# A GNN layer on one core: seven edge products per tile instead of eight, and another order of VectorE's and GpSimd's work in the first tiles

## The chip, the cores and the metric

The kernel runs on one core of one Trainium2 chip. The metric is the device time of one execution in microseconds (us); lower is better. Three timed runs of the kernel before gave a median of 1362.57 us.

## The reference

Only what sets the shape of the work is kept.

```python
def reference(x, src, dst, edge_attr_64, W1, b1, W2, b2):
    # x: 50000 x 256, edge_attr_64: 25000 x 64, dst sorted; W1: 320 x 512, W2: 512 x 256
    h = jnp.maximum(_layernorm(x, axis=-1), 0.0)
    agg = segment_sum(edge_attr_64, dst, num_segments=50000)
    counts = segment_sum(ones(25000), dst, num_segments=50000)
    agg = agg / jnp.maximum(counts, 1.0)[:, None]
    combined = jnp.concatenate([agg, h], axis=1)
    hidden = jax.nn.relu(combined @ W1 + b1)
    return x + hidden @ W2 + b2
```

So each node gets the mean of its incoming edges (64 wide), beside its normalised features (256 wide), and both go through a two-layer perceptron; the result is added to x.

## The kernel before

**Tiles.** The 50000 nodes are cut into 98 tiles of 512 nodes, each of four groups of 128. All engines' instructions are written out by hand, in one program per engine, with semaphores between them. Tiles 0, 1 and the start of tile 2 are unrolled; from tile 2 to tile 95 a loop runs two tiles (`step(2i)`, `step(2i+1)`) per pass, and the last two tiles are unrolled again. Buffers of a tile come in pairs (b = 0 or 1), those after the transposition (HT, QA, QB, H1) exist once.

**Precision.** Every product is made of fp32r operands split into a high and a low part: a value is rounded to fp32r (`_hi`), and the rest is kept beside it (`_lo`). A product a·b is hi·hi + lo·hi + hi·lo.

**One tile on TensorE (PE).** `step(t)` issues, for each of the four slices m of the hidden layer, six products of 512 columns from the node features (`layer1_nodes`, L884 to L886) and two from the edge means (`layer1_means`, L893 and L894). Between m = 1 and m = 2 stand the edge products of the next tile, `edge_means(t+1)`, L873 and L874: for each group k of 128 nodes, a one-hot matrix OH (which of the 128 edges in a window goes to which of 128 nodes) is multiplied with E_hi and with E_lo, 64 columns of weights and 128 moving columns each. Both accumulate into rows 0 to 63 of the bank PA; that makes eight products. Then `layer2` issues 16 pairs (L907 with 512 columns, L909 with 256); the first six pairs need the slices m = 0 to 2 of the hidden layer, the seventh needs m = 3. In the steps of tiles 0 and 1 the edge products of the next tile stand inside `layer2`, behind the eighth pair, and not between the slices.

**What the means pass through.** ScalarE (ACT) rounds PA into QB (L587) and copies that into rows 0 to 63 of QA (L589). VectorE (DVE) writes the rest, PA − QB, into rows 64 to 127 of QA (L711, `means_low`), and the semaphore s_qlo tells TensorE that L893 may start.

**Where the other operands come from.** SyncE (SP) loads x and the edge windows: per tile, eight small transfers whose places it reads from a table of addresses (L308 into ER, L309 into DT). VectorE computes the windows' relative targets (`ends`, L651) and four one-hots (`onehot`, L813). GpSimd (POOL) scales the edges (L427, into ES), ScalarE rounds them (L576, E_hi) and GpSimd subtracts (L432, E_lo). ScalarE normalises x (L570); SP then moves the result into four quadrants with four transfers (L275, HQ, called `move`), VectorE transposes it in two halves (L699), ScalarE and VectorE split it (L582, L707). In a step VectorE transposes the first half of tile t+1 before it makes the low part of slice m = 3 of tile t (`hidden_low`, L715), which the seventh pair of `layer2` needs. At the end it makes the outputs (`residual`, L726 and L729) of each group of nodes. GpSimd adds the bias to x for a later tile (`residual_in`, L438, 128x1024).

**What sets the order.** Each engine takes its instructions strictly as written; a wait holds all behind it. SP's program in the first tiles is: windows of tile 2, `move(2)`, windows of tile 3, store of tile 0, x of tile 4, windows of tile 4, `move(3)`, store of tile 1, x of tile 5, windows of tile 5, `move(4)`. VectorE's order for tile 1 ends with: transposition of tile 2, `residual(1, 0)`, `residual(1, 1)`, `means_low(2)`, `residual(1, 2)`, `residual(1, 3)`, then `ends(3)` and `onehot(3)`. The wait that stands before the edge products of a tile on TensorE is this:

```python
pe.wait_ge(s_oh, SUB * t + SUB)   # all four one-hots of tile t
pe.wait_ge(s_elo, t + 1)          # its E_lo
```

The functions that the change touches, with the line numbers of the profile:

Of the kernel before, what the change touches and what calls it, by code (L numbers as in the profile page):

```python
# [5 lines left out]
ALU = mybir.AluOpType  # L6
ACT = mybir.ActivationFunctionType
# [7 lines left out]
P = 128  # L15
SUB = 4
# [10 lines left out]
def build(nc, x, src, dst, edge_attr, w1, b1, w2, b2, out):  # L27
# [41 lines left out]
    with ExitStack() as ctx:  # L69
        def sb(name, shape, dt=F32):  # L70
            return ctx.enter_context(nc.sbuf_tensor(name, shape, dt))
# [4 lines left out]
        def sem(name):  # L76
            return ctx.enter_context(nc.semaphore(name))
# [57 lines left out]
        rel = [sb(f"rel{b}", [P, SUB]) for b in range(2)]  # L135

        ES = [sb(f"ES{b}", [P, SUB, DE]) for b in range(2)]
        E_hi = [sb(f"E_hi{b}", [P, SUB, DE], F32R) for b in range(2)]
        E_lo = [sb(f"E_lo{b}", [P, SUB, DE], F32R) for b in range(2)]
        OH = [sb(f"OH{b}", [P, SUB, P], F32R) for b in range(2)]  # L140
        HT = sb("HT", [P, CD, TILE])
        HT_hi = sb("HT_hi", [P, CD, TILE], F32R)
# [46 lines left out]
        def groups(t):  # L189

            return range(GROUPS if isinstance(t, int) and t == TILES - 1 else SUB)
# [46 lines left out]
        s_hhi = sem("s_hhi")  # L238
        s_hlo = sem("s_hlo")
        s_qhi = sem("s_qhi")  # L240
        s_qlo = sem("s_qlo")
        s_l1 = sem("s_l1")
        s_1hi = sem("s_1hi")
# [167 lines left out]
        def _(pool):  # L411
# [17 lines left out]

            def edges_low(t, b):  # L430
                pool.wait_ge(s_ehi, t + 1)
                pool.tensor_tensor(E_lo[b][:], ES[b][:], E_hi[b][:], ALU.subtract).then_inc(s_elo, 1)  # L432

            def residual_in(t, b):

                past(pool, s_fin, SUB * (t - 1))
                pool.wait_ge(s_x[b], 16 * (t // 2 + 1) if isinstance(t, int) else 8 * t + (16 - 8 * b))
                pool.tensor_tensor(XB[b][:], X[b][:], b2_row[:].unsqueeze(1).to_broadcast([P, SUB, D]),  # L438
                                   ALU.add).then_inc(s_xb, 1)
# [97 lines left out]
            edges_low(1, 1)  # L537
            edges_scaled(2, 0)
            edges_low(2, 0)
            residual_in(2, 0)  # L540
            norm(3, 1)
            edges_scaled(3, 1)
            edges_low(3, 1)
            residual_in(3, 1)
            with pool.Fori(1, TILES // 2 - 1) as i:
                for h in range(2):
# [6 lines left out]
        @block.scalar  # L553
        def _(act):
            act.dma_start(X[0][:], x[0:TILE, :].rearrange("(j p) d -> p j d", p=P)).then_inc(s_x[0], 16)
            for q in range(QN):
                act.dma_start(w1_raw[q * QP:(q + 1) * QP, :, :],
                              w1[DE + q * QF:DE + (q + 1) * QF, :].rearrange("(c f) h -> f c h", f=QP)).then_inc(s_w[0], 16)
            act.dma_start(b2_row[:], b2.rearrange("(o d) -> o d", o=1).to_broadcast([P, D])).then_inc(s_b2, 16)

            def layernorm(t, b, js=range(SUB)):

                past(act, s_hq[b], moved(t - 2, b))
                act.wait_ge(s_norm, t + 1)
                for j in js:
                    rows, into = X[b][:, j, :], HN[b][:, j, :]
                    if isinstance(t, int) and t == 0:
                        rows = rows.rearrange("p (q c f) -> p q c f", q=QN, c=CD)
                        into = into.rearrange("p (c q f) -> p q c f", q=QN, c=CD)
                    act.activation(into, rows, ACT.Relu, bias=shift[b][:, j:j + 1],  # L570
                                   scale=rstd[b][:, j:j + 1]).then_inc(s_ln, 1)

            def edges_high(t, b):
                act.wait_ge(s_es, t + 1)
                past(act, s_sum, t - 1)
                act.activation(E_hi[b][:], ES[b][:], ACT.Copy).then_inc(s_ehi, 1)  # L576

            def transposed_high(t):
                past(act, s_l1, CH * t)
                for c in range(CD):  # L580
                    act.wait_ge(s_th, 2 * t + c + 1)
                    act.activation(HT_hi[:, c, :], turned(t, c), ACT.Copy).then_inc(s_hhi, 1)  # L582

            def means_high(t):
                past(act, s_l1, CH * t)
                act.wait_ge(s_sum, t + 1)
                act.activation(QB[0:DE, :], PA[0:DE, :], ACT.Copy).then_inc(s_qhi, 1)  # L587
                act.wait_ge(s_qhi, 2 * t + 1)
                act.activation(QA[0:DE, :], QB[0:DE, :], ACT.Copy).then_inc(s_qhi, 1)  # L589

            def hidden_high(t):
                for m in range(CH):
                    act.wait_ge(s_l1, CH * t + m + 1)
                    if m == 0:
                        past(act, s_l2, SUB * t)
                    act.activation(H1_hi[:, m, nodes(t)], bank(m)[:, nodes(t)], ACT.Relu).then_inc(s_1hi, 1)  # L596

            act.wait_ge(s_rise, 1)
            act.activation(alike[:, 1:WIDE], rise[:], ACT.Relu, bias=ones_f[0:EP, :], scale=-1.0).then_inc(s_alike, 1)
            act.wait_ge(s_w[0], 16 * QN)  # L600
            act.activation(w1_hi[:], w1_raw[:], ACT.Copy).then_inc(s_whi, 1)
            act.wait_ge(s_w[1], 32)
            act.activation(wa_hi[:], wa_raw[:], ACT.Copy).then_inc(s_whi, 1)
            act.wait_ge(s_w[2], 32)
            act.activation(b1_hi[DE:P, :], b1_raw[DE:P, :], ACT.Copy).then_inc(s_whi, 1)
            act.activation(wb_lo[64:96, :], b1_raw[64:96, :], ACT.Copy).then_inc(s_whi, 1)
            layernorm(0, 0)
            transposed_high(0)
            act.wait_ge(s_w[3], 32)
            act.activation(w2_both[:, :, 0, :], w2_raw[:], ACT.Copy).then_inc(s_whi, 1)  # L610
            layernorm(1, 1)
            edges_high(0, 0)
            means_high(0)
            hidden_high(0)
            edges_high(1, 1)
            layernorm(2, 0)
            transposed_high(1)
            means_high(1)
            edges_high(2, 0)
            hidden_high(1)  # L620
            transposed_high(2)
            means_high(2)
            layernorm(3, 1)
            edges_high(3, 1)
            with act.Fori(1, TILES // 2 - 1) as i:
                for h in range(2):
                    hidden_high(2 * i + h)
                    transposed_high(2 * i + (h + 1))
                    means_high(2 * i + (h + 1))
                    layernorm(2 * i + (h + 2), h)  # L630
                    edges_high(2 * i + (h + 2), h)
            hidden_high(TILES - 2)
            transposed_high(TILES - 1)
            means_high(TILES - 1)
            hidden_high(TILES - 1)
# [3 lines left out]
        def _(dve):  # L639
# [68 lines left out]

            def means_low(t):
                dve.wait_ge(s_qhi, 2 * t + 1)  # L710
                dve.tensor_tensor(QA[DE:P, :], PA[0:DE, :], QB[0:DE, :], ALU.subtract).then_inc(s_qlo, 1)  # L711

            def hidden_low(t, m):
                dve.wait_ge(s_1hi, CH * t + m + 1)
# [122 lines left out]
            transpose(2, 0, 0)  # L837
            transpose(2, 0, 1)
            transposed_low(2)
            residual(1, 1, 0)  # L840
            residual(1, 1, 1)
            means_low(2)
            residual(1, 1, 2)
            residual(1, 1, 3)
            ends(3, 1)
            onehot(3, 1)
            with dve.Fori(1, TILES // 2 - 1) as i:
                for h in range(2):
                    step(2 * i + h, h)
# [5 lines left out]
        def _(pe):  # L855
# [10 lines left out]
            def edge_means(t, b):  # L866
                pe.wait_ge(s_oh, SUB * t + SUB)
                pe.wait_ge(s_elo, t + 1)
                past(pe, s_qhi, 2 * t)
                past(pe, s_qlo, t)  # L870
                for k in groups(t):
                    cols = slice(k * P, (k + 1) * P)
                    pe.matmul(PA[0:DE, cols], E_hi[b][:, k, :], OH[b][:, k, :], start=(k == 0), stop=False)  # L873
                    last = pe.matmul(PA[0:DE, cols], E_lo[b][:, k, :], OH[b][:, k, :], start=False, stop=(k == groups(t)[-1]))  # L874
                last.then_inc(s_sum, 1)

            def layer1_nodes(t, m):
# [38 lines left out]
            def step(t, b, later=True):  # L916
                for m in range(CH):
                    if not (isinstance(t, int) and t == 0):
                        layer1_nodes(t, m)
                    layer1_means(t, m)  # L920
                    if m == 1 and later and not (isinstance(t, int) and t < 2):
                        edge_means(t + 1, 1 - b)
                layer2(t)

            pe.wait_ge(s_start, 1)
# [19 lines left out]
            layer1_nodes(0, 2)  # L945
            layer1_nodes(0, 3)
            edge_means(0, 0)
            pe.wait_ge(s_wlo, 2)
            pe.wait_ge(s_ones, 1)
            pe.wait_ge(s_wblo, 2)  # L950
            pe.wait_ge(s_whi, 5)
            step(0, 0)
            step(1, 1)
            with pe.Fori(1, TILES // 2 - 1) as i:
# [26 lines left out]
```

## Time and profile before

| | us |
|---|---|
| median of 3 runs | 1362.57 (1361.99 to 1363.06) |
| the profiled execution, its time | 1361.83 |
| its span, first to last instruction | 1360.0 |
| TensorE busy in it | 1333.9 |
| VectorE busy | 1194.1 |
| ScalarE busy | 695.4 |
| GpSimd busy | 539.7 |
| mean granted TensorE clock | 0.999 of full |

All times of the sections below are counted from the first instruction of the span. "Busy" of TensorE counts matmuls whose ends are modelled and overlap, so its use is better read from the distance between the starts of two matmuls than from the duration of one. "Idle before" names the time that an engine stood still before an instruction, and the engine and tile that released it.

### The profile page before, as it was taken

How to read it: one execution, taken by the hardware profiler on the slowest of the kernel's cores; microseconds unless marked ns; L12 is line 12 of the kernel's file. 1: busy time of each engine (PE TensorE's matmuls, PEld its weight loads, DVE VectorE, ACT ScalarE, POOL GpSimd, SP SyncE). 2: the span in 40 equal slices, each digit the busy share in tenths (PEclk: the TensorE clock that was granted, in tenths of full speed). 3: DMA queues.
4: the chain of work that ended last, by engine and by line, in shares of the span. 5: the costliest groups of instructions: out<-in, count | busy, mean ns of one | idle time of the engine just before them, and what ended most of it. 6: DMA issues, size and time to landing. Idle time of an engine off the chain costs nothing.

```text
span 1360.0 us, 29811 instructions
## 1 busy us (share of the span) xinstructions
PE 1333.9 (98%) x7066; PEld 1118.8 (82%) x7066; DVE 1194.1 (88%) x2961; ACT 695.4 (51%) x1281; POOL 539.7 (40%) x710
## 2 busy tenths in 40 slices
PE   4899999999999999999999999999999999999999
PEld 2688888888888888888888888888888888888887
DVE  5989898988888898989898989898889888989897
ACT  3445555555555454545454545454545454545553
POOL 6333343434343434343434343434343434343431
PEclk9999999999999999999999999999999999999999
DMA  4455555555454545454545464545454545555542
GB/s 112 111 127 120 133 121 130 126 126 130 121 132 120 132 120 133 119 136 115 140 112 143 109 147 107 145 108 143 111 141 112 139 114 137 116 135 118 133 111 74
DMA packets 422724, 168.59 MB, mean 124 GB/s; under 512 B 321188, under 2 KB 422326, under 8 KB 422712
## 3 DMA queue, kind: packets, MB, share of 16 engines
q1 hardware_dynamic: 421720, 167.28, 51.2%
q10 hardware_dynamic: 992, 1.18, 0.3%
q14 instruction: 9, 0.07, 0.0%
q8 instruction: 3, 0.05, 0.0%
HBM read 66.12 MB, written 51.40 MB: 86 GB/s over the span
## 4 chain that ended last, share of the span: by engine, by line
PE 95%; DVE 3%; DMA 1%; POOL 1%; issue 0%; ACT 0%; POOLq 0%; DVEq 0%; SPq 0%
PE P L907 26%; PE P L909 13%; PE P L884 13%; PE P L886 13%; PE P L885 13%; PE P L893 6%; PE P L894 6%; PE PA L873 2%; PE PA L874 2%; DVE H_lo L715 0%; DMA dst_w<-in_dst_dram 0%; DVE OH L813 0%; DVE below L670 0%; DVE stats L645 0%; DVE HT L699 0%
## 5 line engine op out<-in xcount | busy, mean ns | idle before, releaser
L907 PE MATMUL P<-w_both,H_hi 128*128 128x512 f32 x1564 | 557.6, 397 | 1.1 <-DVE H_lo L715 1.0
L596 ACT ACTIVATE H_hi<-P 128x512 fp32r<-128x512 f32 x392 | 233.1, 596 | 513.4 <-PE P L894 513.4
L909 PE MATMUL P<-w_both,H_lo 128*128 128x256 f32 x1564 | 439.6, 281 | 0.0
L715 DVE SCALAR_TENSOR_TENSOR H_lo<-P,H_hi 128x512 fp32r<-128x512 f32 x392 | 268.0, 685 | 113.2 <-ACT H_hi L596 103.2
L907 PEld LDWEIGHTS P<-w_both,H_hi 128*128 128x128 f32 x1564 | 293.7, 188 | 74.8 <-DVE H_lo L715 3.4
L884 PE MATMUL P<-HT_hi,w_hi 128*128 128x512 f32 (+1 forms) x784 | 314.4, 401 | 1.9 <-ACT w_both L610 1.9
L886 PE MATMUL P<-HT_hi,w_lo 128*128 128x512 f32 (+1 forms) x784 | 308.9, 394 | 0.0
L885 PE MATMUL P<-HT_lo,w_hi 128*128 128x512 f32 (+1 forms) x784 | 306.0, 390 | 0.0
L909 PEld LDWEIGHTS P<-w_both,H_lo 128*128 128x128 f32 x1564 | 293.4, 188 | 3.7
L438 POOL TENSOR_TENSOR XB<-X,b_row 128x1024 f32<-128x1024 f32 x98 | 236.8, 2416 | 135.5 <-DVE O L729 135.3
L432 POOL TENSOR_TENSOR E_lo<-ES,E_hi 128x256 fp32r<-128x256 f32 x98 | 73.2, 747 | 400.6 <-ACT E_hi L576 400.6
L699 DVE STREAM_TRANSPOSE HT<-HQ 128x512 f32<-128x512 f32 x194 | 209.3, 1080 | 0.0
L570 ACT ACTIVATE HN<-X,shift,rstd 128x256 f32<-128x256 f32 x392 | 202.4, 587 | 8.3 <-POOL shift L421 8.3
L582 ACT ACTIVATE HT_hi<-HT 128x512 fp32r<-128x512 f32 x194 | 122.9, 633 | 116.4 <-DVE HT L699 116.4
L729 DVE TENSOR_TENSOR O<-P,XB 128x256 f32<-128x256 f32 x391 | 166.0, 425 | 13.3
L886 PEld LDWEIGHTS P<-HT_hi,w_lo 128*128 128x128 f32 x784 | 147.8, 188 | 34.0
L884 PEld LDWEIGHTS P<-HT_hi,w_hi 128*128 128x128 f32 x784 | 148.2, 189 | 29.6 <-ACT w_both L610 2.3
L885 PEld LDWEIGHTS P<-HT_lo,w_hi 128*128 128x128 f32 x784 | 148.7, 190 | 25.3
L726 DVE TENSOR_TENSOR XB<-P,XB 128x256 f32<-128x256 f32 x391 | 163.5, 418 | 4.6 <-PE P L909 1.5
L893 PE MATMUL P<-QA,wa_hi 128*128 128x512 f32 x392 | 153.4, 391 | 1.6 <-POOL w_both L534 1.6
L894 PE MATMUL P<-QB,wb_lo 128*128 128x512 f32 x392 | 152.9, 390 | 0.0
L707 DVE TENSOR_TENSOR HT_lo<-HT,HT_hi 128x512 fp32r<-128x512 f32 x194 | 134.9, 695 | 15.4 <-ACT HT_hi L582 9.2
(74 smaller groups left out, 1140.0 us busy)
## 6 DMA issues: line engine op xcount, KB each, us to landing
HQ<-HN SPq DMA_DIRECT2D x388, 128.0 KB, 3.1
out_dram<-O SPq DMA_DIRECT2D x97, 512.0 KB, 3.3
X<-in_x_dram SPq DMA_DIRECT2D x96, 512.0 KB, 3.6
ER<-in_edge_attr_dram SPq DMA_DIRECT2D x392, 32.0 KB, 1.8
DT<-table_dram SPq DMA_DIRECT2D x392, 1.0 KB, 1.7
X<-in_x_dram ACTq DMA_DIRECT2D x1, 512.0 KB, 5.0
w_raw<-in_L_gnn_W_dram ACTq DMA_DIRECT2D x4, 128.0 KB, 5.2
w_raw<-in_L_gnn_W_dram SPq DMA_DIRECT2D x2, 256.0 KB, 4.0
```

Of the source, the lines that this page charges most:

```text
L438: pool.tensor_tensor(XB[b][:], X[b][:], b2_row[:].unsqueeze(1).to_broadcast([P, SUB, D]), ALU.add).then_inc(s_xb, 1)
L570: act.activation(into, rows, ACT.Relu, bias=shift[b][:, j:j + 1], scale=rstd[b][:, j:j + 1]).then_inc(s_ln, 1)
L596: act.activation(H1_hi[:, m, nodes(t)], bank(m)[:, nodes(t)], ACT.Relu).then_inc(s_1hi, 1)
L699: dve.transpose(HT[:, c, :].rearrange("p (j n k) -> p k j n", j=SUB, k=QN), HQ[b][:, :, c * QP:(c + 1) * QP].rearrange("p (k j) f -> p k j ...
L715: dve.scalar_tensor_tensor(out=H1_lo[:, m, nodes(t)], in0=bank(m)[:, nodes(t)], scalar=0.0, in1=H1_hi[:, m, nodes(t)], op0=ALU.max, op1=AL ...
L884: pe.matmul(bank(m)[:, nodes(t)], w1_hi[:, c, cols], HT_hi[:, c, nodes(t)], start=(c == 0), stop=False)
L885: pe.matmul(bank(m)[:, nodes(t)], w1_hi[:, c, cols], HT_lo[:, c, nodes(t)], start=False, stop=False)
L886: pe.matmul(bank(m)[:, nodes(t)], w1_lo[:, c, cols], HT_hi[:, c, nodes(t)], start=False, stop=False)
L893: pe.matmul(bank(m)[:, nodes(t)], wa_hi[:, cols], QA[:, nodes(t)], start=False, stop=False)
L894: pe.matmul(bank(m)[:, nodes(t)], wb_lo[:, cols], QB[:, nodes(t)], start=False, stop=True).then_inc(s_l1, 1)
L907: pe.matmul(out_bank(j)[some, :], H1_hi[:, m, rows], w2_both[:, m, :, :].rearrange("p a d -> p (a d)"), start=(m == 0), stop=False)
L909: last = pe.matmul(out_bank(j)[some, 0:D], H1_lo[:, m, rows], w2_both[:, m, 0, :], start=False, stop=(m == CH - 1))
```

## The change

**E_hi and E_lo become one tile.** E_both holds, for each group, 64 columns of the high part and next to them 64 of the low part. ScalarE and GpSimd write the two halves where they wrote the two tiles. For group 0 one product with 128 columns of weights replaces two with 64: its sum of the high part lands in rows 0 to 63 of PA and that of the low part in rows 64 to 127. The other three groups keep their two products. So a tile has seven edge products.

**The low part of group 0 is added on VectorE.** Behind L711 `means_low` gets a second instruction, over rows 64 to 127 and the 128 columns of group 0: QA = PA + QA. It waits for a new semaphore, s_qpart, which L711 raises; s_qlo is raised by the second instruction now.

**The first tiles.** GpSimd waits for the one-hots of tile 2 before `residual_in(2)`, and for those of tile 3 before `residual_in(3)`. On VectorE `ends(3)` and `onehot(3)` go ahead of all of tile 1's residuals, and `means_low(2)` goes ahead of the second. TensorE's wait for the split W2 moves from before the first use of QA to before `layer2(0)`.

```diff
-        E_hi = [sb(f"E_hi{b}", [P, SUB, DE], F32R) for b in range(2)]
-        E_lo = [sb(f"E_lo{b}", [P, SUB, DE], F32R) for b in range(2)]
+        E_both = [sb(f"E_both{b}", [P, SUB, 2, DE], F32R) for b in range(2)]
...
-                pool.tensor_tensor(E_lo[b][:], ES[b][:], E_hi[b][:], ALU.subtract).then_inc(s_elo, 1)
+                pool.tensor_tensor(E_both[b][:, :, 1, :], ES[b][:], E_both[b][:, :, 0, :], ALU.subtract).then_inc(s_elo, 1)
...
             edges_low(2, 0)
+            pool.wait_ge(s_oh, 3 * SUB)
             residual_in(2, 0)
             norm(3, 1)
             edges_scaled(3, 1)
             edges_low(3, 1)
+            pool.wait_ge(s_oh, 4 * SUB)
             residual_in(3, 1)
...
-                act.activation(E_hi[b][:], ES[b][:], ACT.Copy).then_inc(s_ehi, 1)
+                act.activation(E_both[b][:, :, 0, :], ES[b][:], ACT.Copy).then_inc(s_ehi, 1)
...
             def means_low(t):
                 dve.wait_ge(s_qhi, 2 * t + 1)
-                dve.tensor_tensor(QA[DE:P, :], PA[0:DE, :], QB[0:DE, :], ALU.subtract).then_inc(s_qlo, 1)
+                dve.tensor_tensor(QA[DE:P, :], PA[0:DE, :], QB[0:DE, :], ALU.subtract).then_inc(s_qpart, 1)
+                dve.wait_ge(s_qpart, t + 1)
+                dve.tensor_tensor(QA[DE:P, 0:P], PA[DE:P, 0:P], QA[DE:P, 0:P], ALU.add).then_inc(s_qlo, 1)
...
             transposed_low(2)
+            ends(3, 1)
+            onehot(3, 1)
             residual(1, 1, 0)
+            means_low(2)
             residual(1, 1, 1)
-            means_low(2)
             residual(1, 1, 2)
             residual(1, 1, 3)
-            ends(3, 1)
-            onehot(3, 1)
...
-                for k in groups(t):
+                pe.matmul(PA[:, 0:P], E_both[b][:, 0, :, :].rearrange("p a d -> p (a d)"), OH[b][:, 0, :],
+                          start=True, stop=True)
+                for k in groups(t)[1:]:
                     cols = slice(k * P, (k + 1) * P)
-                    pe.matmul(PA[0:DE, cols], E_hi[b][:, k, :], OH[b][:, k, :], start=(k == 0), stop=False)
-                    last = pe.matmul(PA[0:DE, cols], E_lo[b][:, k, :], OH[b][:, k, :], start=False, stop=(k == groups(t)[-1]))
+                    pe.matmul(PA[0:DE, cols], E_both[b][:, k, 0, :], OH[b][:, k, :], start=(k == 1), stop=False)
+                    last = pe.matmul(PA[0:DE, cols], E_both[b][:, k, 1, :], OH[b][:, k, :], start=False,
+                                     stop=(k == groups(t)[-1]))
...
+                if isinstance(t, int) and t == 0:
+                    pe.wait_ge(s_whi, 5)
+                    pe.wait_ge(s_wlo, 2)
                 layer2(t)
...
             edge_means(0, 0)
-            pe.wait_ge(s_wlo, 2)
             pe.wait_ge(s_ones, 1)
             pe.wait_ge(s_wblo, 2)
-            pe.wait_ge(s_whi, 5)
             step(0, 0)
```

Two places of the order, as the programs have them. The first is VectorE at the end of tile 1, from the low part of slice m = 3 on (P11 is that slice's bank; P20 and P21 hold the outputs of groups 0 and 1). Before:

```order
L715 SCALAR_TENSOR_TENSOR H1_lo<-P11,H1_hi 128x512
L699 STREAM_TRANSPOSE HT<-HQ0 128x4x128 x2
L707 TENSOR_TENSOR HT_lo<-HT,HT_hi 128x512 x2
L726 TENSOR_TENSOR XB1<-P20,XB1 128x256
L729 TENSOR_TENSOR O1<-P20,XB1 128x256
L726 TENSOR_TENSOR XB1<-P21,XB1 128x256
L729 TENSOR_TENSOR O1<-P21,XB1 128x256
L711 TENSOR_TENSOR QA<-PA,QB 64x512
```

And now, the same place of VectorE's program (its line numbers are higher by 2 to 4):

```order
L719 SCALAR_TENSOR_TENSOR H1_lo<-P11,H1_hi 128x512
L701 STREAM_TRANSPOSE HT<-HQ0 128x4x128 x2
L709 TENSOR_TENSOR HT_lo<-HT,HT_hi 128x512 x2
L653 TENSOR_TENSOR rel1<-DT1,base 128x4
L817 TENSOR_SCALAR OH1<-iota_row,rel1 128x128 x4
L730 TENSOR_TENSOR XB1<-P20,XB1 128x256
L733 TENSOR_TENSOR O1<-P20,XB1 128x256
L713 TENSOR_TENSOR QA<-PA,QB 64x512
L715 TENSOR_TENSOR QA<-PA,QA 64x128
```

The targets and the four one-hots of tile 3 stand ahead of the residuals now, one residual pair fewer stands before the subtraction into QA, and the addition over 64x128 follows it.

The second place is TensorE in the loop, from the end of slice m = 1 on (OH1 and E_hi1 are those of the next tile). Before:

```order
L893 MATMUL P13<-QA,wa_hi 128x512
L894 MATMUL P13<-QB,wb_lo 128x512
L867 ISA
L868 REGISTER_ALU
L24 REGISTER_ALU
L873 MATMUL PA<-OH1,E_hi1 64x128
L874 MATMUL PA<-OH1,E_lo1 64x128
```

And now:

```order
L900 MATMUL P13<-QA,wa_hi 128x512
L901 MATMUL P13<-QB,wb_lo 128x512
L871 ISA
L872 REGISTER_ALU
L24 REGISTER_ALU
L875 MATMUL PA<-OH1,E_both1 128x128
L879 MATMUL PA<-OH1,E_both1 64x128
L880 MATMUL PA<-OH1,E_both1 64x128
```

The product with 128 columns of weights comes first, right behind a product of 512 moving columns; six of 64 columns follow it, where eight stood.

## Rows read from the trace of the kernel before

**Rows 1.** The page: busy time of each engine, share of the span, instructions.

```profile
PE 1333.9 (98%) x7066; PEld 1118.8 (82%) x7066; DVE 1194.1 (88%) x2961; ACT 695.4 (51%) x1281; POOL 539.7 (40%) x710
```

**Rows 2.** Busy time in one steady tile (start:end, length, then each engine's).

```profile
699.38:712.91 13.53, 13.53 (x74) 11.40 (x73) 11.98 (x31) 7.06 (x15) 5.36 (x7) 1.00 0.52 126
```

**Rows 3.** Timeline (start, duration, us), TensorE and its loads around a tile's edge products.

```profile
702.23 0.39 PE L894 MATMUL P<-QB,wb_lo 128*128 128x512 f32 x1
702.45 0.22 PE L873 MATMUL PA<-OH,E_hi 128*64 128x128 f32 x1
702.46 0.14 PEld L874 LDWEIGHTS PA<-OH,E_lo 128*64 128x64 f32 x1
...
702.52 0.14 PEld L873 LDWEIGHTS PA<-OH,E_hi 128*64 128x64 f32 x1
...
702.88 0.19 PEld L884 LDWEIGHTS P<-HT_hi,w_hi 128*128 128x128 f32 x1
702.93 0.45 PE L884 MATMUL P<-HT_hi,w_hi 128*128 128x512 f32 x1
...
703.22 0.39 PE L885 MATMUL P<-HT_lo,w_hi 128*128 128x512 f32 x1
```

**Rows 4.** Timeline: VectorE's wait in a steady tile, its subtraction, TensorE's load behind it.

```profile
705.66 0.69 DVE L715 SCALAR_TENSOR_TENSOR H_lo<-P,H_hi 128x512 fp32r<-128x512 f32 x1 [1.02 <-ACT H_hi L596]
...
712.22 0.69 DVE L711 TENSOR_TENSOR QA<-PA,QB 64x512 fp32r<-64x512 f32 x1
...
713.46 0.19 PEld L893 LDWEIGHTS P<-QA,wa_hi 128*128 128x128 f32 x1
```

**Rows 5.** L711 alone (ns min/median/max, first and last start); L729 by line (busy, mean ns).

```profile
L711 DVE TENSOR_TENSOR QA<-PA,QB x98: 683/684/685, 33.5 to 1346.7; 64x512 fp32r<-64x512 f32 x98
L729 DVE TENSOR_TENSOR O<-P,XB 128x256 f32<-128x256 f32 x390 | 165.6, 425 | 13.3
```

**Rows 6.** Timeline: one-hots on VectorE, GpSimd's bias addition, tiles 2 and 3, one steady.

```profile
46.88 3.57 DVE L813 TENSOR_SCALAR OH<-iota_row,rel 128x128 fp32r<-128x128 f32 x4
47.60 2.46 DVE L813 TENSOR_SCALAR OH<-iota_row,rel 128x128 fp32r<-128x128 f32 x1
47.55 2.42 POOL L438 TENSOR_TENSOR XB<-X,b_row 128x1024 f32<-128x1024 f32 x1
62.06 3.00 DVE L813 TENSOR_SCALAR OH<-iota_row,rel 128x128 fp32r<-128x128 f32 x4
710.53 0.87 DVE L813 TENSOR_SCALAR OH<-iota_row,rel 128x128 fp32r<-128x128 f32 x4
```

**Rows 7.** Timeline: TensorE in tiles 0 to 3, where it waits or changes pace.

```profile
34.41 0.47 PE L893 MATMUL P<-QA,wa_hi 128*128 128x512 f32 x1 [1.60 <-POOL w_both L534]
54.67 0.50 PE L907 MATMUL P<-w_both,H_hi 128*128 128x512 f32 x1 [0.70 <-DVE H_lo L715]
60.31 0.50 PE L893 MATMUL P<-QA,wa_hi 128*128 128x512 f32 x1
62.48 0.39 PE L894 MATMUL P<-QB,wb_lo 128*128 128x512 f32 x1
65.40 0.24 PE L873 MATMUL PA<-OH,E_hi 128*64 128x128 f32 x1 [2.53 <-DVE OH L813]
68.92 0.63 PE L884 MATMUL P<-HT_hi,w_hi 128*128 128x512 f32 x1
69.35 0.63 PE L885 MATMUL P<-HT_lo,w_hi 128*128 128x512 f32 x1
71.23 0.39 PE L907 MATMUL P<-w_both,H_hi 128*128 128x512 f32 x1
```

**Rows 8.** HQ of tile 3: SP's issues (ns each, first and last start), landing, VectorE's transposition.

```profile
L275 SPq DMA_DIRECT2D HQ<-HN x4: 625/636/677, 63.0 to 65.1; - x4
DMA to landing us min/median/max: 3.0/3.2/3.3
70.85 1.09 DVE L699 STREAM_TRANSPOSE HT<-HQ 128x512 f32<-128x512 f32 x1
```

More of the change, by code:

```diff
@@ L240, in build @@
         s_qhi = sem("s_qhi")
+        s_qpart = sem("s_qpart")
         s_qlo = sem("s_qlo")
```

## The prediction

> **What bounds the kernel now.** I read the page first: TensorE is busy for 98% of the span, VectorE for 88% [rows 1]. A busy share alone would not settle it, so I took the stretches next: in a steady tile of 13.53 us TensorE has no gap, while VectorE works 11.98 us [rows 2]. The timeline of one tile shows it product by product: each starts as soon as the one before has streamed [rows 3]. So from about tile 4 on only two things change the time: TensorE's own work, and a wait that reaches it. In the first tiles it is different: there TensorE stands still for VectorE several times [rows 7], and an operand that comes earlier is worth its whole lead, until the next late one.
>
> **The merged product, steady tiles.** The eight edge products start at 702.45 and the product behind them at 702.93, so one costs 0.48 / 8 = 0.060 us [rows 3]. The change drops one. Does the wider load of the merged product cost anything? A load of 128 columns behind a short product does: L884, loaded at 702.88, is followed by L885 only 0.29 us after it, while the product behind L894, also of 512 columns, starts 0.22 after it; so about 0.06 us stand uncovered [rows 3]. But the merged product is the first of its group and its load runs beside L894 with 512 columns, as those of all other wide products do; the load behind it is 64 wide, as now, and L884 pays its 0.06 as now. I take the full 0.060 us saved. The bounds are 0 (an uncovered 0.06 eats it) and 0.06. Tiles 4 to 97 are 94: 94 × 0.060 = **5.6 us less**.
>
> The Trainium skill ("TensorE: Matmul & The Clock Gate", section "LDWEIGHTS (loading the stationary operand)") says that a load costs by its columns, P / 1.2 ns: 107 ns for the merged one and 53 ns for each that it replaces, so where loads set the pace the merger saves nothing. By that the term would be 0 and not 5.6 us. The trace agrees that loads of 64 columns come every 0.06 us, as the products do [rows 3], so it does not tell which of the two sets that pace.
>
> **The added addition on VectorE.** 64x512 takes 684 ns and 128x256 takes 425 [rows 5], both with one operand in PSUM. The slope is 259 / 256 = 1.01 ns a column, so 128 columns come to 425 − 130 = 0.295 us, and about 0.03 us for its wait on the instruction before. Bounds: 0.22 us (a one-hot of 128 columns, 0.87 / 4 [rows 6]) and 0.68 us (the whole L711 again). I take 0.33, because both rows of this kind of instruction lie on that line. What it delays: L711 ends at 712.91 and TensorE loads for L893 at 713.46, 0.55 us later [rows 4]; in all steady tiles the timeline has this same distance to 0.02. So 0.22 us remain and TensorE does not wait. Behind it on VectorE stand three residual pairs, the first low part and two statistics; all start up to 0.33 us later. VectorE catches up where it now waits 1.02 us for ScalarE [rows 4]. TensorE's next needs of them (output banks of groups 2 and 3) have over a microsecond in the same timeline; GpSimd's bias addition and SP's store go later by the same 0.33 us, in front of waits that SP has anyway. Cost: nothing, as long as the 0.55 and the 1.02 us are there.
>
> The strided writes of E_both on ScalarE and GpSimd change no element count; I cost them at nothing, covered by the more than 1.5 us that E_lo lies ahead of its use.
>
> **The first tiles, step by step** (all places in time of the trace of before).
>
> 1. Tile 0. L893 was held until 34.41 by the split of W2 [rows 7]. That wait is moved behind it, but the first L711 starts at 33.5 [rows 5], so QA was ready only at 34.15 and is now ready at 34.48. **+0.1 us**: the moved wait gives nothing.
> 2. One-hots of tile 2. Four take 3.57 us, and one of them 2.46 us: exactly while GpSimd's bias addition of 2.42 us runs; undisturbed, four take 0.87 [rows 6]. GpSimd's subtraction still holds the first until 47.60, so they end at about 48.45 and not 50.45: VectorE is 2.0 us ahead. The seventh pair of `layer2(1)` started at 54.67, late by VectorE [rows 7]; it starts at about 52.75. **−1.9 us.** GpSimd's addition starts 0.9 us later, with nothing waiting for it soon.
> 3. QA of tile 2. It came just before L893, at 60.26 [rows 7], and L893 could have started at 60.20. Now it has 2.0 us of lead and 0.8 more (a residual pair goes behind it), but targets and one-hots (1.0) and the addition (0.33) go before it: 58.8. TensorE wants it at 60.20 − 2.0 = 58.2. A new stall of **+0.6**.
> 4. One-hots of tile 3. TensorE waited from 62.71 (62.48 and one product of 0.23) until 65.40, 2.7 us, since they came last and again took 3.00 us [rows 6, 7]. They are done by 57.2 now. **−2.7 us**; at slice m = 2 of tile 2 the sum is 0.1 − 1.9 + 0.6 − 2.7 − 0.1 (merged products of tiles 1 and 3) = −4.1 or so.
> 5. The clock. Behind that stall the products start 0.43 us apart and not 0.23 [rows 7]: the granted clock is at its lower level, 1.2 GHz, for about eight products. 8 × 0.20 = **−1.6 us** if it stays at 2.4 GHz. Sum −5.7: `layer2(2)`, at 71.23 before [rows 7], is wanted at 65.5 and its seventh pair at 67.6.
> 6. What is late next: HQ of tile 3. SP issues these four transfers from 63.01 on, right behind the windows of tile 4, with no wait, so SP's own row of instructions sets the time, and nothing in the change moves it. The last is issued at 65.1 and lands 3.2 us later, 68.3 [rows 8]. VectorE must transpose (1.1) before it makes the low part of m = 3 (0.7): 70.1. TensorE stands still for about 2.5 us: **+2.5**. Sum −3.2.
> 7. The clock again. In these tiles the stall of 1.6 us before 34.41 was not followed by the lower clock and the one of 2.7 us was [rows 7]. 2.5 is nearer the second, so I take **+1.6**; bounds 0 and 1.6. Sum **−1.7** for the first tiles (−3.2 at the other end).
>
> Behind this `move(4)` goes earlier too and VectorE's next tiles find their inputs; I see nothing that takes the rest.
>
> **The sum.** 1361.83 (the profiled execution's own time: span 1360.0 and 1.8 around it) − 5.6 − 1.7 = **1354.5 us**; 1353.0 with no second fall of the clock. The median of the runs shown is 0.7 above that execution; on its scale the two are 1355.2 and 1353.7.
>
> **The rivals.**
>
> *A: loads set the pace of edge products.* Then two 64-column loads are as dear as one of 128 and the steady tiles save nothing. For it: loads and products both come each 0.06 us. Against it: the merged load lies beside 512 columns. 1361.8 − 1.7 to 3.2 = 1358.6 to 1360.1. Chance 0.10.
>
> *B: QA comes too late in every tile; slower.* The place is L893 of slice m = 0. It decides from the point where the added instruction and its wait take more than 0.55 us. At the upper bound, 0.68 + 0.03, the stall is 0.16 us, and a load that nothing covers costs 0.11 more (at 60.31, where the product that follows starts 0.34 behind and not 0.23). Less 0.06 saved, +0.21 a tile: 1361.8 + 94 × 0.21 − 1.7 = 1380. [...] Against it: both rows of such instructions give half that. Chance 0.08.
>
> *C: the first tiles give nothing.* The lead of step 4 is lost at HQ and at a stall after it, only the steady tiles gain: 1356.2. For it: SP's queue is full through tile 5. Chance 0.09.
>
> *D: HQ of tile 3 comes in time* (SP or its transfers go faster), all 5.7 us stay: 1350.5. Against it: the row of issues on SP has no slack. Chance 0.05.
>
> **How the numbers follow.** The forecast, with either outcome of the clock, has 0.68 and its own range 1352 to 1356.5. The range 1351 to 1359 adds C and part of A, and leaves out B, D and the rest of A, 0.17 in all. A measurement of this kernel can tell about 0.2%, 2.7 us: faster means below 1359.8. Forecast, C, D and 0.06 of A are faster, 0.88; 0.04 of A is the same; B is slower, 0.08.
>
> **What would show it.** Right: seven edge products in 0.42 us and steady tiles of 13.46 us; an addition of about 0.3 us on VectorE and no idle time of TensorE before L893's successor; one-hots of tiles 2 and 3 in about 0.9 us; TensorE's longest stall before the seventh pair of tile 2, released by VectorE behind a wait for HQ. Wrong: steady tiles still of 13.52 (A); idle time before the first product with QA in each tile (B); no wait for HQ in tile 3 (D); a new stall behind tile 3 (C).

## The result and the profile after

The changed kernel takes 1355.09 us (median of 5 runs, 1353.04 to 1355.85), the one before 1362.57 (1361.99 to 1363.06): ratio 0.9948, 95% interval 0.9937 to 0.9959, so 7.5 us less, of which the interval leaves 5.6 to 8.6. The prediction said 1354.5, in 1351 to 1359, and faster with 0.88. The total is right; its two terms, the steady tiles and the first ones, were not of the predicted sizes.

The page of the changed kernel, its busy times (share of the span, instructions), answers to [rows 1]; its profiled execution took 1355.23 us, span 1353.3, so 6.6 and 6.7 less than that of before:

```profile
span 1353.3 us, 29713 instructions
...
PE 1326.5 (98%) x6968; PEld 1119.2 (83%) x6968; DVE 1209.9 (89%) x3059; ACT 695.7 (51%) x1281; POOL 541.3 (40%) x710
```

TensorE still fills 98% of the span, with 98 products fewer; VectorE has 98 instructions more and 15.8 us more of work.

**Steady tiles.** The timeline of TensorE around the edge products, the place of [rows 3]:

```profile
712.55 0.39 PE L901 MATMUL P<-QB,wb_lo 128*128 128x512 f32 x1
712.77 0.22 PE L875 MATMUL PA<-OH,E_both 128*128 128x128 f32 x1
712.83 0.22 PE L879 MATMUL PA<-OH,E_both 128*64 128x128 f32 x1
...
713.13 0.22 PE L880 MATMUL PA<-OH,E_both 128*64 128x128 f32 x1
713.19 0.44 PE L891 MATMUL P<-HT_hi,w_hi 128*128 128x512 f32 x1
713.47 0.39 PE L892 MATMUL P<-HT_lo,w_hi 128*128 128x512 f32 x1
```

Seven products take 0.42 us, and the merged one with 128 columns of weights costs the same 0.06 as each of the others. The first product behind them is followed after 0.28 and not 0.29. The period of a tile (the time from one tile to the next), from the starts of VectorE's subtraction into QA in tile 4 and tile 94, fell from 13.520 to 13.447 us. This view of VectorE and of TensorE's loads, the place of [rows 4], shows the margin that is left:

```profile
709.03 0.69 DVE L713 TENSOR_TENSOR QA<-PA,QB 64x512 fp32r<-64x512 f32 x1
709.75 0.29 DVE L715 TENSOR_TENSOR QA<-PA,QA 64x128 fp32r<-64x128 f32 x1
...
710.26 0.19 PEld L900 LDWEIGHTS P<-QA,wa_hi 128*128 128x128 f32 x1
```

The addition starts 0.03 us after the end of the subtraction, takes 0.29 and ends 0.22 us before the load that it releases. That is the 0.33 and the 0.22 of the prediction.

**First tiles.** TensorE where it waits or changes pace, the places of [rows 7] (in brackets the idle time before, and who ended it):

```profile
35.30 0.56 PE L900 MATMUL P<-QA,wa_hi 128*128 128x512 f32 x1 [1.93 <-DVE QA L715]
36.09 0.63 PE L900 MATMUL P<-QA,wa_hi 128*128 128x512 f32 x1
36.51 0.63 PE L901 MATMUL P<-QB,wb_lo 128*128 128x512 f32 x1
60.85 0.50 PE L900 MATMUL P<-QA,wa_hi 128*128 128x512 f32 x1 [0.73 <-DVE QA L715]
71.98 0.50 PE L914 MATMUL P<-w_both,H_hi 128*128 128x512 f32 x1 [2.31 <-DVE H_lo L719]
73.16 0.63 PE L914 MATMUL P<-w_both,H_hi 128*128 128x512 f32 x1
73.80 0.63 PE L914 MATMUL P<-w_both,H_hi 128*128 128x512 f32 x1
```

Neither the wait before the seventh pair of tile 1 nor that for the one-hots of tile 3 is there any more. In their place stands the one at 71.98, and the timeline of VectorE says why:

```profile
49.32 0.88 DVE L817 TENSOR_SCALAR OH<-iota_row,rel 128x128 fp32r<-128x128 f32 x4
58.09 0.88 DVE L817 TENSOR_SCALAR OH<-iota_row,rel 128x128 fp32r<-128x128 f32 x4
70.33 1.08 DVE L701 STREAM_TRANSPOSE HT<-HQ 128x512 f32<-128x512 f32 x1 [2.88 <-DMA HQ<-HN]
```

The view of one tile, HQ, from 60 to 72 us, has SP's issues (median ns of one, first and last start) and the time from issue to landing:

```profile
L275 SPq DMA_DIRECT2D HQ<-HN x4: 625/654/1832, 64.3 to 66.4; - x4
...
DMA to landing us min/median/max: 3.0/3.6/3.9
```

The first starts at 64.3, where [rows 8] had 63.0. The last starts at 66.4, holds SP for 1.83 us and lands 3.9 us after its start, at 70.3; step 6 of the prediction had 68.3. The one-hots of tiles 2 and 3 take 0.88 us, where [rows 6] had 3.57 and 3.00; VectorE then stands still 2.88 us for the transfers. Two stretches of the granted clock (PEclk, the third number from the end) belong to the doubled distances: behind the stall in tile 0, and behind that in tile 2.

```profile
35.50:38.90 3.40, 3.40 (x9) 2.64 (x9) 1.62 (x3) 1.81 (x4) 2.29 (x2) 0.51 0.55 95
73.20:76.50 3.30, 3.30 (x12) 2.81 (x12) 3.06 (x9) 3.27 (x7) 0.00 (x0) 0.50 0.14 21
```

0.5 is the lower level, 1.2 GHz. From the starts of each tile's first product (tile 0: 24.47 before, 25.08 after) the first tiles read as follows.

| tile | before, us | after, us | difference | of it predicted |
|---|---|---|---|---|
| 0 | 18.81 | 19.90 | +1.09 | +0.1 |
| 1 | 15.54 | 13.60 | −1.94 | −1.9 |
| 2 | 18.05 | 18.54 | +0.49 | about +0.3 |
| 3 | 13.52 | 13.44 | −0.08 | −0.06 |

The sum is −0.44 where the prediction had −1.7 (its own terms add up to −1.5). From tile 4 to the end the span has 1262.7 us (1353.3 − 90.56) and had 1269.6 (1360.0 − 90.39): −6.9 where it had −5.6. The remaining +0.6 stands before the first product of tile 0 and is no effect that can be put down to the change: over all traces of this document that product starts between 23.9 and 25.6 us.

### The profile page after: what moved, and what is told of

Its sections match the earlier page's. It is cut to its first block, busy times and chain, and to the rows that moved or that the text cites. A ratio compares the mean times of both kernels' runs of the same rounds, so it can differ in the third digit from the quotient of the medians.

```text
span 1353.3 us, 29713 instructions
## 1 busy us (share of the span) xinstructions
PE 1326.5 (98%) x6968; PEld 1119.2 (83%) x6968; DVE 1209.9 (89%) x3059; ACT 695.7 (51%) x1281; POOL 541.3 (40%) x710
## 4 chain that ended last, share of the span: by engine, by line
PE 94%; SPq 2%; POOL 1%; DMA 1%; issue 1%; DVE 1%; ACT 0%; POOLq 0%; DVEq 0%
PE P L914 27%; PE P L916 13%; PE P L891 13%; PE P L893 13%; PE P L892 13%; PE P L900 6%; PE P L901 6%; PE PA L880 1%; PE PA L879 1%; SPq L307 0%; SPq L309 0%; DMA dst_w<-in_dst_dram 0%; PE PA L875 0%; SPq L308 0%; SPq L275 0%
## 5 line engine op out<-in xcount | busy, mean ns | idle before, releaser
L893 PE MATMUL P<-HT_hi,w_lo 128*128 128x512 f32 (+1 forms) x784 | 308.0, 393 | 0.0
L432 POOL TENSOR_TENSOR E_both<-ES,E_both 128x256 fp32r<-128x256 f32 x98 | 73.0, 745 | 403.5 <-ACT E_both L578 403.5
L893 PEld LDWEIGHTS P<-HT_hi,w_lo 128*128 128x128 f32 x784 | 147.6, 188 | 32.5
```

Source lines behind the costliest of these rows:

```text
L893: pe.matmul(bank(m)[:, nodes(t)], w1_lo[:, c, cols], HT_hi[:, c, nodes(t)], start=False, stop=False)
```

## The experiments

The kernel before was timed again beside each group of experiments, with medians of 1362.6, 1361.1, 1361.3 and 1361.0. Each row is therefore read against its own.

| kernel | median, us | ratio to before (95% interval) | us to before |
|---|---|---|---|
| the change | 1355.09 | 0.9948 (0.9937 to 0.9959) | −7.5 |
| the change, run again | 1353.05 | 0.9939 (0.9925 to 0.9952) | −7.9 |
| merge_only | 1356.14 | 0.9961 (0.9948 to 0.9974) | −5.0 |
| start_only | 1360.67 | 0.9997 (0.9988 to 1.0005) | −0.4 |
| merged_last | 1358.30 | 0.9981 (0.9972 to 0.9989) | −2.8 |
| two_additions | 1355.24 | 0.9962 (0.9949 to 0.9975) | −5.9 |
| three_additions | 1366.91 | 1.0040 (1.0025 to 1.0056) | +5.6 |
| move3_act | 1350.65 | 0.9921 (0.9908 to 0.9935) | −10.6 |
| no_pool_waits | 1352.66 | 0.9937 (0.9924 to 0.9951) | −8.6 |
| fill_tile0 | 1355.13 | 0.9957 (0.9944 to 0.9971) | −6.2 |
| old_order_move3 | 1356.22 | 0.9962 (0.9948 to 0.9976) | −4.8 |
| fill_move3 | 1350.42 | 0.9922 (0.9908 to 0.9935) | −10.6 |
| best | 1349.77 | 0.9916 (0.9902 to 0.9929) | −11.2 |

### The change once more

> The changed kernel once more, on the chip of the three runs beside it, for comparison: 1355, with or without the lower clock after the stalls of 1.9 and 2.3 us in tiles 0 and 2 (1.6 us each).

Measured: 1353.05, 7.9 us under the kernel before beside it, against 7.5 the first time. Its trace has the 1.93 us of idle time in tile 0 with the lower clock behind it, and in tile 2 a stall of 2.51 us with no lower clock behind it, where the first trace had 2.31 with one.

### The two parts alone

merge_only is the change with VectorE's, GpSimd's and TensorE's old order in the first tiles:

```diff
             transposed_low(2)
-            ends(3, 1)
-            onehot(3, 1)
             residual(1, 1, 0)
-            means_low(2)
             residual(1, 1, 1)
+            means_low(2)
             residual(1, 1, 2)
             residual(1, 1, 3)
+            ends(3, 1)
+            onehot(3, 1)
...
-            pool.wait_ge(s_oh, 3 * SUB)
...
-            pool.wait_ge(s_oh, 4 * SUB)
```

> The merged product and its addition alone, with the order of the first tiles as before. My theory: steady tiles of 13.45 us as in the changed kernel, 94 x 0.07 = 6.8 us less than before, and first tiles as before: 1362.6 - 6.8 = about 1356. The rival that loads set the pace (A): steady tiles of 13.52, about 1362.6.

Measured: 1356.14, 5.0 us under before, and a period of 13.45 us. Rival A falls. That it is 5.0 and not 6.8 lies for the most part in tile 0, which took 19.82 us against 18.81: the longer stall for QA is there too, 1.93 us, and the lower clock behind it.

start_only is the kernel before with the new order alone (the diff is the inverse of the above, on eight edge products).

> The order of the first tiles alone, with eight edge products and no addition. By the prediction: 1.7 to 3.2 us less than before, 1359.4 to 1360.9, with a stall of about 2.5 us before the seventh pair of tile 2, behind VectorE's wait for HQ of tile 3. Rival C (the first tiles give nothing): 1362.6.

Measured: 1360.67, with 11 runs from 1358.1 to 1363.4: 0.4 us under before, not told from none, and short of the 1.7 to 3.2 that I expected. In its profiled execution the stall before the seventh pair of tile 2 was there as predicted, 2.21 us, and tile 3 starts 50.80 us after tile 0's first product where it started 52.40 after it before, 1.6 us less. One execution of a kernel that scatters over 5 us does not carry more than that. The rows of its TensorE:

```profile
35.18 0.47 PE L895 MATMUL P<-QA,wa_hi 128*128 128x512 f32 x1 [1.60 <-DVE QA L713]
...
70.55 0.50 PE L909 MATMUL P<-w_both,H_hi 128*128 128x512 f32 x1 [2.21 <-DVE H_lo L717]
```

The first row also settles the moved wait for the split W2: without it the stall in tile 0 is the same 1.60 us, and it is QA that ends it. The profile of before named GpSimd's split, which ended at 34.31, within 0.2 us of QA at 34.15. From the end of QA to TensorE's start lie 0.26 us in both traces (34.15 to 34.41, 34.92 to 35.18).

### What sets the pace of an edge product

```diff
-                pe.matmul(PA[:, 0:P], E_both[b][:, 0, :, :].rearrange("p a d -> p (a d)"), OH[b][:, 0, :],
-                          start=True, stop=True)
                 for k in groups(t)[1:]:
...
+                last = pe.matmul(PA[:, 0:P], E_both[b][:, 0, :, :].rearrange("p a d -> p (a d)"), OH[b][:, 0, :],
+                                 start=True, stop=True)
                 last.then_inc(s_sum, 1)
```

> The merged product of each tile is issued last of the seven and not first, so its wide load and the wide load behind it both run beside products of 128 columns. My theory: the merged product's own load now stands uncovered by 0.06 us, the product saved is given back: steady tiles of 13.50 to 13.51, about 5.6 us slower than the changed kernel, 1360.7. Rival: products alone set the pace and the width of the load does not matter: 1355.1, no difference.

Measured: 1358.30, 2.8 us under before where the change is 7.5 and 7.9 under it: 4.7 to 5.1 us slower (5.6 was expected). Its period is 13.507, 0.060 above the change's 13.447. The timeline of its TensorE at the end of the group:

```profile
713.81 0.22 PE L878 MATMUL PA<-OH,E_both 128*64 128x128 f32 x1
713.87 0.28 PE L880 MATMUL PA<-OH,E_both 128*128 128x128 f32 x1
713.99 0.44 PE L891 MATMUL P<-HT_hi,w_hi 128*128 128x512 f32 x1
714.26 0.39 PE L892 MATMUL P<-HT_lo,w_hi 128*128 128x512 f32 x1
```

Behind the merged product it takes 0.12 us to the next start, where a product behind a 64-column load takes 0.06. So behind a product of 128 moving columns the wide load costs 0.06 us more than a narrow one; in steady tiles most of the merger's gain comes from its place at the head of the group, beside 512 columns. The Trainium skill ("TensorE: Matmul & The Clock Gate", section "LDWEIGHTS (loading the stationary operand)") prices a load by its columns; the estimates worked out from its formula, P / 1.2 ns, are 107 ns for 128 columns and 53 for 64. The 0.12 here agrees with the first, plus some 10 ns. The 0.06 agrees with the second, but a product of 128 moving columns might set it as well. The rule spoke against the merger; in merged_last most of the gain is indeed gone, and with the merged product first the load beside 512 columns costs nothing that shows.

### How much the addition may take (rival B)

```diff
+                dve.tensor_tensor(spare[DE:P, :], PA[DE:P, 0:P], QB[DE:P, 0:P], ALU.add)
                 dve.tensor_tensor(QA[DE:P, 0:P], PA[DE:P, 0:P], QA[DE:P, 0:P], ALU.add).then_inc(s_qlo, 1)
```

> A second instruction of the shape of the addition (64x128, one operand in PSUM, into a scratch tile) before the one that releases TensorE; the output stays the same. Rival B's point: VectorE's work between L713 and the release passes the 0.22 us that are left. Expected 0.29 more: QA 0.07 us late, plus 0.11 for a load that nothing covers, 0.1 to 0.2 us a tile, 9 to 19 us: 1364 to 1374. If the release hid behind the load in flight the time would stay at 1355.

Measured: 1355.24, 5.9 us under the kernel before: by the medians no difference from the change that can be told. The expectation of 1364 to 1374 missed, and the timeline of the trace says why (the scratch instruction is the first of the two):

```profile
708.79 0.29 DVE L716 TENSOR_TENSOR spare<-PA,QB 64x128 fp32r<-64x128 f32 x1
709.00 0.29 DVE L717 TENSOR_TENSOR QA<-PA,QA 64x128 fp32r<-64x128 f32 x1
...
709.34 0.19 PEld L902 LDWEIGHTS P<-QA,wa_hi 128*128 128x128 f32 x1
```

The instruction that waits for nothing starts 0.21 us after the one before it, not 0.29. So the release came just in time: the load starts 0.05 us behind it. The period is 13.465, 0.019 above the change, which over 94 tiles is 1.8 us; the traces show this small loss though the medians do not tell it. One more of the same:

> Two instructions of the addition's shape before the one that releases TensorE. With one, its release came 0.05 us before the load and steady tiles took 13.465 us; one more costs 0.21 as it does not wait. Rival B's price: release 0.16 us late plus up to 0.11 for the uncovered load: 0.16 to 0.27 us a tile, 15 to 25 us, 1370 to 1380, and idle time of TensorE before its first product with QA in every tile.

Measured: 1366.91, 5.6 us above before, ratio 1.0040. The timeline of VectorE's last addition and of what waits for it, and below it the waits of the steady tiles:

```profile
702.39 0.29 DVE L718 TENSOR_TENSOR QA<-PA,QA 64x128 fp32r<-64x128 f32 x1
...
702.73 0.19 PEld L903 LDWEIGHTS P<-QA,wa_hi 128*128 128x128 f32 x1 [0.29 <-DVE QA L718]
702.74 0.50 PE L903 MATMUL P<-QA,wa_hi 128*128 128x512 f32 x1
```

```profile
PEld P L903 <- DVE QA L718: 26.2, 91, 0.3
```

TensorE's load stands 0.29 us in every tile. The period is 13.590, 0.143 above the change, and 94 times that is 13.4 us: 13.1 and 13.5 by the differences in the table (5.6 + 7.5 and 5.6 + 7.9). That is under the 0.16 that I gave as the least, and the 1366.9 is under the 1370 to 1380. The product that waited starts 0.26 us behind the one before it and is followed after 0.33, where 0.23 is usual: the 0.03 and the 0.10 make up most of the loss. Rival B is therefore real. It begins where the 0.22 us of margin are used up, less the 0.05 between a release and its load.

### What became of the lead (step 6)

```diff
             load_windows(4, 0)
-            move(3, 1)
             store(1, 1)
...
             layernorm(3, 1)
             edges_high(3, 1)
+            act.wait_ge(s_ln, SUB * 3 + SUB)
+            into_quadrants(act, 1)
```

> The changed kernel with the four transfers of HQ of tile 3 issued by ScalarE behind its rounding of the edges of tile 3, at about 61 us of the span, and not by SP behind the windows of tile 4 (64.3). Step 6 (HQ late by SP's queue): HQ lands near 66.5, VectorE no longer waits for it, TensorE's stall of 2.3 us before the seventh pair of tile 2 goes, and with it the lower clock that follows: 2.3 to 4 us less than the changed kernel, 1351 to 1353. Rival: another operand is late right behind, under 1 us less.

Measured: 1350.65, 10.6 us under before and about 3 under the change, a little better than the 1351 to 1353 expected. ScalarE's queue issues HQ of tile 3 (view of the tile HQ), some 4 us earlier:

```profile
L275 ACTq DMA_DIRECT2D HQ<-HN x4: 646/662/717, 60.7 to 62.8; - x4
```

VectorE's first transposition of it, in its timeline, now waits for nothing:

```profile
68.36 1.11 DVE L702 STREAM_TRANSPOSE HT<-HQ 128x512 f32<-128x512 f32 x1
```

Is that the lead of the new order, or would early transfers help any order? The same edit on merge_only:

> The merged product with the order of the first tiles as before (as in the run merge_only), and HQ of tile 3 issued by ScalarE. If HQ was the only thing that swallowed the lead of the new order, then here, where nothing waits for HQ, its earlier issue gives nothing: 1356, as merge_only; and the distance to move3_act (1350.7) is the full worth of the new order, about 5.5 us as steps 2 to 5 of the prediction have it (5.7). Rival: issuing HQ early helps any order, about 1352.

Measured: 1356.22, as merge_only. The early transfers alone give nothing. With them the new order is worth 10.6 − 4.8 = 5.8 us, and steps 2 to 5 of the prediction had 5.7 (with 0.1 for tile 0). The medians alone give this only to some 2.5 us, but the two traces agree: from the first product of tile 0 to that of tile 4 they take 61.66 and 67.43 us, 5.77 apart. So the order does what it was credited with, and the late HQ from SP's queue takes most of it away. The other test of the same step takes out the two waits of GpSimd:

```diff
-            pool.wait_ge(s_oh, 3 * SUB)
             residual_in(2, 0)
...
-            pool.wait_ge(s_oh, 4 * SUB)
             residual_in(3, 1)
```

> The changed kernel without GpSimd's two waits for the one-hots. The prediction's step 2: the one-hots of tile 2 take 3.0 to 3.6 us again and the seventh pair of tile 1 comes 1.9 us later. But by step 6 HQ of tile 3 does not come later, so TensorE's stall before the seventh pair of tile 2 shrinks from 2.3 to under 1 us: start of tile 3 unchanged, total within 1 us of the changed kernel, or 1.6 less where the lower clock no longer follows that stall. Rival: the two leads add up, 1.9 us slower.

Measured: 1352.66, 8.6 us under before: not slower than the change (7.5 and 7.9 under). Four one-hots take 3.07 us again, beside GpSimd's addition of 2.42:

```profile
49.11 3.07 DVE L815 TENSOR_SCALAR OH<-iota_row,rel 128x128 fp32r<-128x128 f32 x4
...
49.08 2.42 POOL L438 TENSOR_TENSOR XB<-X,b_row 128x1024 f32<-128x1024 f32 x1 [0.30 <-DVE O L731]
```

VectorE came later by this, and then waited 0.20 us for HQ and not 2.88; TensorE did not stand before the seventh pair of tile 2 at all, and its clock stayed up there. With SP as it is, GpSimd's waits are worth nothing.

The traces show one thing more here that the prediction left out. From the issue of the first HQ transfer of tile 3 on SP to the landing of the last it takes 5.3 to 5.4 us in the three traces without GpSimd's waits (before, merge_only, no_pool_waits), and 5.7 to 6.7 in the seven with them and HQ on SP's queue (the change 6.0, in its other trace 6.6). In four of the seven one of the four issues holds SP for 1.2 to 1.8 us, where 0.6 to 0.7 is usual. So part of the wait for HQ comes together with GpSimd's waits and is not only SP's place in line, and that they are worth nothing here may be due to it; what holds the transfers is not shown.

### The clock in tile 0

```diff
             edge_means(0, 0)
+            for i in range(6):
+                pe.matmul(PS[:].rearrange("p a b -> p (a b)"), w1_hi[:, 0, 0:P], HT_hi[:, 0, :], start=True, stop=True)
             pe.wait_ge(s_ones, 1)
```

> The changed kernel with six products of 512 columns (result unused, into a bank that is free by then) issued in the 1.9 us in which TensorE waits for QA of tile 0. They take 1.4 us and end before QA is there. Theory: the stall of 1.93 us is what the lower clock of 3.4 us behind it follows; filled, the products of layer 1 and 2 of tile 0 start 0.23 apart and tile 3 starts 1.6 us earlier in executions that had that fall: 1353.5. Rival: the clock falls in tile 0 for another reason (which part of the stretch a check falls on), no difference.

Measured: 1355.13, no gain over the change, and not the 1353.5 expected. Its two stretches show the full clock in tile 0 behind the filled gap, and the lower one in tile 2:

```profile
35.00:40.00 5.00, 4.37 (x19) 3.02 (x19) 3.33 (x9) 3.71 (x9) 3.43 (x3) 1.00 0.64 164
68.00:78.00 10.00, 6.71 (x25) 5.53 (x24) 6.77 (x15) 4.64 (x9) 1.84 (x4) 0.67 0.50 126
```

TensorE stood 0.50 us in tile 0 and not 1.93, reached tile 2 earlier, and then stood 3.29 us behind the wait for HQ, whose last transfer landed at 70.9. The granted clock of 0.67 over those 10 us means that about 6.6 of them were at the lower level, against 3.4 in the change. Over the kernels' traces: in the nine with the addition and nothing in the gap, the stall in tile 0 is 1.93 us or more, and the products behind it run at the lower clock in each. In the two without the addition (before, start_only) it is 1.60 and they do not; in the three with the gap filled it is 0.5, and they do not. With HQ out of the way the filled gap should count:

> Both: six unused products in tile 0's wait, and HQ of tile 3 issued by ScalarE. With fill_tile0 alone the earlier tile 0 ran into the same HQ. Here the 1.6 us of the lower clock in tile 0 should arrive: 1349.0, against 1350.7 for move3_act. If it stays at 1350.7, another operand with a fixed time (SP's or GpSimd's) bounds the first tiles.

Measured: 1350.42, against 1350.65 for move3_act: the 1.6 us did not arrive in the median, though its profiled execution was never at the lower clock in the first tiles and its span was 1348.2 where that of move3_act was 1350.0. Most of that difference of 1.8 us lies before the first product of tile 0 (24.21 and 25.58 us); from there to the first product of tile 4 it is 61.26 against 61.66, 0.4 us. The gain of 1.6 was put too high. From the end of the stall in tile 0 to the first product of tile 1 TensorE took 9.68 us in the change and 9.60 in move3_act, and 8.83 and 8.82 with the gap filled. So the lower clock in tile 0 cost about 0.8 us and not 1.6. In the kernel before, at the full clock, the first pairs of `layer2(0)` start 0.60 us apart (36.52, 37.12, 37.72) and the later ones 0.35, so some of the slower products fill time in which TensorE was held up in any case. Of the 0.8 another 0.4 is lost on the way to tile 4; where is not shown.

### A version that beats both

fill_move3 and one more edit on VectorE:

```diff
             transposed_low(2)
+            means_low(2)
             ends(3, 1)
             onehot(3, 1)
             residual(1, 1, 0)
-            means_low(2)
```

> As fill_move3, and VectorE makes QA of tile 2 right behind the transposed low halves, ahead of the targets, the one-hots and the first residual. QA comes 1.8 us earlier, the stall of 0.7 to 0.9 us before the first product with QA of tile 2 goes, the one-hots are still in time for their products: 1348.2.

Measured: 1349.77 (1349.40 to 1350.06), 11.2 us under before, ratio 0.9916 (0.9902 to 0.9929), and 3.3 under the change run beside it, whose ratio to before was 0.9939 (0.9925 to 0.9952). The waits of TensorE's products from 30 to 100 us are down to two:

```profile
PE P L901 <- DVE QA L716: 0.5, 1, 0.5
PE P L915 <- DVE H_lo L720: 0.3, 1, 0.3
```

The stall for QA of tile 2 is gone, as expected, but the time is 1.6 us above the 1348.2 expected; the last edit by itself is not told from none by the medians.

## Why the prediction was right, and where a term was off

- **The merged product**: right in mechanism, sized at 0.060 us a tile; it is 0.073, and 94 tiles make 6.9 us and not 5.6. The group itself gives 0.060 in the mean of 84 steady tiles. The rest, about 0.013, is mostly spread over the remainder of the tile; what makes it is not shown.
- **The addition**: 0.29 + 0.03 as worked out from the slope of two rows, 0.22 us of margin left as worked out, no wait in steady tiles. The loss starts near where rival B put it; its price was put at 0.27 a tile for 0.16 us too late, and 0.14 was measured with about 0.2 too late by the same count (0.33 and two more of 0.21, against 0.55).
- **Step 1, tile 0, was the step that failed.** It said +0.1 us; the tile became 1.09 longer. I took GpSimd's split of W2 for what released L893, since the profile named it, and let it cover most of the addition. start_only shows that QA was the last, so the whole 0.33 is added to the stall: 1.60 to 1.93. And step 7 asked only of the stall in tile 2 whether the clock would fall. It fell behind the 1.93 us in tile 0 too, which cost about 0.8 us; with the gap filled it did not.
- **Steps 2 to 5**: tile 1 lost 1.94 us of the 1.9 predicted, the one-hots take 0.88 each time, the new stall for QA of tile 2 is 0.73 and not 0.6, and with HQ out of the way the order is worth 5.8 us where these steps had 5.7.
- **Step 6**: the stall before the seventh pair of tile 2 is there, 2.31 us against 2.5, released by VectorE behind a wait for HQ. The mechanism is right, the size is luck: the last transfer landed at 70.3 and not 68.3, and TensorE wanted the pair at 69.7 (71.98 − 2.31) and not 67.6, so both came 2 us later. "Nothing in the change moves it" was wrong by the longer time from issue to landing, 3.9 us for the last transfer and not 3.2; the rest of the 2 us is the later start of the issues.
- **Step 7**: the lower clock followed it in the profiled execution. It did not in the change's other trace (idle 2.51 us, products behind it 0.24 apart), so both ends of that term happen, and runs of one kernel can differ by it.

The errors of +1.3 in the first tiles and −1.3 in the steady ones cancel. That the median fell so near the forecast is in part this luck.

## What to carry to other kernels

Before crediting a lead on the critical engine, follow the same operand chain to the next thing whose time is set elsewhere: here a queue of transfers took much of a lead of 5.8 us, and moving four issues to another engine's queue brought back 3. Where two releasers end within a few tenths of each other, count an addition to either as uncovered. A merged, wider weight load is worth what runs beside it: first behind a long product its load was free, last behind a short one it ate most of the gain.

## What the hardware showed that I had not expected

A VectorE instruction over 64x128 that waits for nothing adds 0.21 us behind one of the same shape, though each lasts 0.29 (two_additions, 708.79 to 709.00); one that waits for its predecessor adds 0.32 (the change, 0.03 and 0.29). And in tile 0 the products behind 1.60 us of idle time went on at the full clock and those behind 1.93 us or more at half of it, in all eleven traces that had one or the other, while stalls of 2.0 to 2.5 us in tile 2 were followed by the lower clock in some executions (2.21 and 2.31) and not in others (2.02 and 2.51).
